# Attention scores without the last key's column, in a key-by-key bank, with a moving operand read by a stride

## The reference

```python
q = split_heads(layernorm(x) @ Wq); k = split_heads(ctx @ Wk); v = split_heads(ctx @ Wv)
attn = softmax(einsum('bhid,bhjd->bhij', q, k) * 64 ** -0.5)          # 77 keys
x = x + tanh(g_xattn[0]) * (merge_heads(attn @ v) @ Wo + bo)
x = x + tanh(g_ffn[0]) * (layernorm(x) @ W[idx] + b[idx])             # one of 8 W, 512 x 512
```

## Time and profile before

| | |
|---|---|
| median of 3 runs | 1053.37 us (1049.84 to 1053.71) |
| profiled execution | 1052.05 us, span 1050.3 us, mean granted TensorE clock 0.998 |
| PE busy | 1035.0 us, 99% of the span, 6065 matmuls |
| DVE busy | 851.7 us, 81% |
| ACT busy | 744.7 us, 71% |
| POOL busy | 438.8 us, 42% |

### The profile page before, as it was taken

The page is one execution under the profiler, slowest core; times in us unless marked ns, Lnnn a source line. Parts: engine busy times, 40 slices in busy tenths (PEclk is TensorE's granted clock), DMA queues, the critical chain, the costliest instruction groups (busy, mean ns, idle before and its releaser), DMA issues.

```text
span 1050.3 us, 21821 instructions
## 1 busy us (share of the span) xinstructions
PE 1035.0 (99%) x6065; PEld 588.1 (56%) x6065; DVE 851.7 (81%) x1800; ACT 744.7 (71%) x2712; POOL 438.8 (42%) x635
## 2 busy tenths in 40 slices
PE   9998899999999999999999999999999999999998
PEld 7634455555555555555555555555555555555555
DVE  4877988888888887888888887888888887888876
ACT  3578887766776677767776677767776676767762
POOL 0575344444433343444433443444433443444322
PEclk9999999999999999999999999999999999999999
DMA  8414466655666656655666656655666656655656
GB/s 312 104 26 107 95 128 133 137 115 117 127 136 135 135 128 134 136 119 110 131 137 135 135 123 139 136 115 110 132 138 137 136 121 135 135 114 113 132 115 141
DMA packets 383639, 135.02 MB, mean 129 GB/s; under 512 B 361728, under 2 KB 363316, under 8 KB 383540
## 3 DMA queue, kind: packets, MB, share of 16 engines
q1 hardware_dynamic: 383476, 134.09, 59.0%
q0 software_dynamic: 64, 0.00, 0.0%
HBM read 27.48 MB, written 16.78 MB: 42 GB/s over the span
## 4 chain that ended last, share of the span: by engine, by line
PE 92%; DVE 4%; ACT 2%; DMA 1%; SPq 1%; issue 1%; POOL 0%; DVEq 0%
PE banks L1356 83%; PE banks L1580 3%; PE banks L1459 1%; PE banks L1386 1%; PE banks L1395 1%; PE banks L1467 1%; ACT work L858 1%; DMA work<-work 1%; DVE vw_area L1062 1%; ACT vw_area L811 1%; PE banks L1448 1%; DVE work L1162 1%; DVE work L425 0%; DMA fold_area<-in_ctx 0%; DVE fold_area L1070 0%
## 5 line engine op out<-in xcount | busy, mean ns | idle before, releaser
L858 ACT ACTIVATE work<-banks,red,cst 128x77 f32<-128x77 f32 x1024 | 410.4, 431 | 89.1 <-DVE red L1153 89.1
L1356 PE MATMUL banks<-fold_area,work 128*128 128x462 f16 (+1 forms) x2304 | 410.6, 336 | 1.4 <-DMA work<-work 0.7
L1356 PE MATMUL banks<-vw_area,work 128*128 128x512 f16 x1674 | 373.1, 380 | 2.6 <-DMA work<-work 2.6
L1356 PEld LDWEIGHTS banks<-fold_area,work 128*128 128x128 f16 x2304 | 223.9, 97 | 176.2 <-DMA work<-work 1.2
L1356 PEld LDWEIGHTS banks<-vw_area,work 128*128 128x128 f16 x1674 | 164.1, 98 | 188.5 <-DMA work<-work 2.9
L425 DVE SCALAR_TENSOR_TENSOR work<-work 128x256 f16<-128x256 f32 (+3 forms) x444 | 240.1, 575 | 3.5 <-ACT work L881 3.0
L858 ACT ACTIVATION_READ_ACCUMULATOR work<-banks,red,cst 128x1 f32 x1024 | 225.7, 220 | 0.0
L1151 DVE TENSOR_REDUCE stats<-banks 128x6 f32<-128x462 f32 (+1 forms) x192 | 112.1, 584 | 109.2 <-PE banks L1356 108.7
L1356 PE MATMUL banks<-work 128*128 128x256 f16 x1302 | 162.4, 272 | 1.6 <-DVE work L1237 1.6
L1356 PEld LDWEIGHTS banks<-work 128*128 128x128 f16 x1302 | 126.7, 98 | 33.4 <-issue 1.3
L703 POOL TENSOR_TENSOR stats<-stats,cst 128x1 f32<-128x1 f32 x64 | 12.5, 196 | 284.7 <-DVE stats L1187 284.7
(11 more groups left out here) (145 smaller groups left out, 814.6 us busy)
## 6 DMA issues: line engine op xcount, KB each, us to landing
work<-in_x SPq DMA_DIRECT2D x64, 256.0 KB, 2.8
out<-work SPq DMA_DIRECT2D x63, 256.0 KB, 2.2
work<-work SPq DMA_TRANSPOSE x254, 3.0
fold_area<-in_L_xattn_Wo SPq DMA_DIRECT2D x4, 512.0 KB, 8.9
work<-in_L_ffn_W SPq DMA_DIRECT2D x2, 1024.0 KB, 6.9
fold_area<-in_L_xattn_Wq SPq DMA_DIRECT2D x2, 1024.0 KB, 12.3
fold_area<-in_L_xattn_Wk SPq DMA_DIRECT2D x2, 768.0 KB, 12.0
fold_area<-in_L_xattn_Wv SPq DMA_DIRECT2D x2, 384.0 KB, 6.2
```

Source lines behind the costliest of these rows:

```text
L858: nc.scalar.activation(probs_of(h, h + 1), s_bank(m, k)[:, (h - h0) * J:(h - h0 + 1) * J], ACT.Exp, bias=nmx[:, h:h + 1], scale=exp_scale, ...
L1356: mm = nc.tensor.matmul(ps, lhs(l), rhs(r), start=first and n == 0, stop=last and n == 2, skip_group_check=onto)
```

## The change

Scores are counted from that of the last key. Before the keys are projected, POOL subtracts the last key's context from that of the 76 others (`ctxT_from_last`), so that `keys_of`, `key_fold` and A carry 76 columns per batch and head in place of 77. The score of the last key is then 0 in every row.

In a score bank the columns now lie key by key: for each key, its 6 (or 4) heads. They end at column 456 in every bank, so that a bank of 4 heads starts at column 152, and columns 456 to 461 of banks 0 to 3 hold zeros, which DVE writes once near the end of the folding. These zeros serve as the last key of all heads. `s_heads` is the view by head of a bank, with its 77 keys. The maxima and the exponentials read through it: successive keys of a head are 6 (or 4) fp32 apart.

A itself stays head by head in SBUF. The score matmul walks it so that its columns come key by key: successive columns are 76 fp16 (152 bytes) apart.

```diff
+    JS = J - 1
+    HS = HEADS * JS
+    BS = B * JS
...
-        a_split = [fold_area[:, k * A_WORDS:(k + 1) * A_WORDS].bitcast(F16)...
+        a_split = [fold_area[:, k * A_WORDS:k * A_WORDS + B * HS].bitcast(F16)...
...
         def s_bank(m, k):
             h0, h1 = BANKS[k]
-            return banks[:, (3 * m + k) % S_BANKS, 0:(h1 - h0) * J]
+            return banks[:, (3 * m + k) % S_BANKS, HB * JS - (h1 - h0) * JS:HB * JS]
+
+        def s_heads(m, k):
+            h0, h1 = BANKS[k]
+            cols = banks[:, (3 * m + k) % S_BANKS, HB * JS - (h1 - h0) * JS:HB * JS + h1 - h0]
+            return cols.rearrange("p (j h) -> p h j", h=h1 - h0)
...
+            for b in range(B):                                     # POOL
+                keys = ctxT[:, :, b * J:(b + 1) * J]
+                pool.wait_ge(ctxT_copied, b + 1)
+                nc.gpsimd.tensor_tensor(ctxT_from_last[:, :, b * JS:(b + 1) * JS], keys[:, :, 0:JS], keys[:, :, JS:J].to_broadcast([P, CT, JS]),
+                                        ALU.subtract).then_inc(ctxT_shifted, 1)
...
-                    nc.scalar.activation(probs_of(h, h + 1), s_bank(m, k)[:, (h - h0) * J:(h - h0 + 1) * J], ACT.Exp,
+                    nc.scalar.activation(probs_of(h, h + 1), s_heads(m, k)[:, h - h0, :], ACT.Exp,
...
+                if (kind, n) == (KEY, UNITS - 3):                  # DVE
+                    assert all(pair_of(KEY, v) >= S_BANKS for v in (UNITS - 2, UNITS - 1))
+                    dve.wait_ge(k_staged, key_staged_before(UNITS))
+                    dve.wait_ge(a_lo, key_highs_after(UNITS - 3))
+                    nc.vector.memset(banks[:, 0:S_BANKS, HB * JS:HB * J], 0.0).then_inc(last_zeroed, 1)
...
-                nc.vector.reduce_max(mx[:, h0:h1], by_head(s_bank(m, k)), AX.X).then_inc(mx_ready, 1)
+                nc.vector.reduce_max(mx[:, h0:h1], s_heads(m, k), AX.X).then_inc(mx_ready, 1)
...
+                if h == 0:                                         # PE, keys_of
+                    pe.wait_ge(ctxT_shifted, B)
-                    mm = nc.tensor.matmul(banks[:, pair_of(PROJECT, h // 2) + h % 2, 0:BJ], wk_raw[:, k, h * P:(h + 1) * P], ctxT[:, k, :],
+                    mm = nc.tensor.matmul(banks[:, pair_of(PROJECT, h // 2) + h % 2, 0:BS], wk_raw[:, k, h * P:(h + 1) * P], ctxT_from_last[:, k, :],
...
-                    nc.tensor.matmul(banks[:, pair_of(KEY, v) + e, 0:BJ], wqT[rows, h, k * P:(k + 1) * P], kT[rows, h, :],
+                    nc.tensor.matmul(banks[:, pair_of(KEY, v) + e, 0:BS], wqT[rows, h, k * P:(k + 1) * P], kT[rows, h, :],
...
+                    if is_tile(o, m, 0) and n == 0:                # PE, scores
+                        pe.wait_ge(last_zeroed, 1)
...
                         mm = split_products(s_bank(m, n), lambda s: turned[:, s, k, :],
-                                            lambda s: a_split[k][:, s, m % B, h0 * J:h1 * J], k == LAST_FOLDED[0], k == LAST_FOLDED[-1])
+                                            lambda s: a_split[k][:, s, m % B, h0 * JS:h1 * JS].rearrange("p (h j) -> p j h", j=JS), k == LAST_FOLDED[0], k == LAST_FOLDED[-1])
```

More of the change, by code:

```diff
@@ L82, in flamingo_layer @@
         fold_area = sb("fold_area", [P, KT * A_WORDS])
-        a_split = [fold_area[:, k * A_WORDS:(k + 1) * A_WORDS].bitcast(F16).rearrange("p (s b n) -> p s b n", s=2, b=B) for k in range(KT)]
+        a_split = [fold_area[:, k * A_WORDS:k * A_WORDS + B * HS].bitcast(F16).rearrange("p (s b n) -> p s b n", s=2, b=B) for k in range(KT)]
         c = Carve(fold_area)
@@ L93, in flamingo_layer @@
         ctxT = c.take(CT * BJ).rearrange("p (k n) -> p k n", k=CT)
+        ctxT_from_last = c.take(CT * BS).rearrange("p (k n) -> p k n", k=CT)
         assert c.at <= 3 * A_WORDS
@@ L153, in flamingo_layer @@
         c.at = folds
-        kT = c.take(HP * BJ).rearrange("p (h n) -> p h n", h=HP)
+        kT = c.take(HP * BS).rearrange("p (h n) -> p h n", h=HP)
         wqT = c.take(HP * D).rearrange("p (h n) -> p h n", h=HP)
-        k_stage = [c.take(2 * BJ).rearrange("p (e n) -> p e n", e=2),
-                   at(D + HP * BJ, 2 * BJ).rearrange("p (e n) -> p e n", e=2)]
-        assert c.at <= x2T_at and D + HP * BJ + 2 * BJ <= RING * D
+        k_stage = [c.take(2 * BS).rearrange("p (e n) -> p e n", e=2),
+                   at(D + HP * BJ, 2 * BS).rearrange("p (e n) -> p e n", e=2)]
+        assert c.at <= x2T_at and D + HP * BJ + 2 * BS <= RING * D
         free = x2T_at + KT * D
@@ L204, in flamingo_layer @@
             sem("ident_zero"), sem("ident_ready"), sem("floor_set"), sem("consts_set"), sem("pads_set"))
-        ctxT_done, ctxT_copied = sem("ctxT_done"), sem("ctxT_copied")
+        ctxT_done, ctxT_copied, ctxT_shifted = sem("ctxT_done"), sem("ctxT_copied"), sem("ctxT_shifted")
         v_done, v_copied, v_scaled, v_scaled_end = sem("v_done"), sem("v_copied"), sem("v_scaled"), sem("v_scaled_end")
@@ L231, in flamingo_layer @@
         s_done, mx_ready, nmx_ready, exp_done = sem("s_done"), sem("mx_ready"), sem("nmx_ready"), sem("exp_done")
+        last_zeroed = sem("last_zeroed")
         rsum_ready, p_ready, p_hi, p_lo, pT_turned, pad_zeroed = (
@@ L393, in pair_banks @@
         def pair_banks(first):
-            return banks[:, first:first + 2, 0:BJ].rearrange("p e (b j) -> p e b j", b=B)
+            return banks[:, first:first + 2, 0:BS].rearrange("p e (b j) -> p e b j", b=B)
         def pair_of_stage(stage):
@@ L402, in pair_of_heads @@
             four, a = h // 2, h % 2
-            cols = a_split[k][:, s, :, 4 * four * J:4 * (four + 1) * J].rearrange("p b (e r j) -> p e b r j", e=2, r=2)
+            cols = a_split[k][:, s, :, 4 * four * JS:4 * (four + 1) * JS].rearrange("p b (e r j) -> p e b r j", e=2, r=2)
             return cols[:, :, :, a, :]
@@ L777, in copy_k @@
                 nc.scalar.copy(kT[:, 2 * n:2 * n + 2, :],
-                               banks[:, pair_of(PROJECT, n):pair_of(PROJECT, n) + 2, 0:BJ]).then_inc(k_copied, 1)
+                               banks[:, pair_of(PROJECT, n):pair_of(PROJECT, n) + 2, 0:BS]).then_inc(k_copied, 1)
             copy_k(0)
@@ L821, in key_high @@
                         act.wait_ge(k_stage_lo, n - 1)
-                    nc.scalar.copy(k_stage[n % 2], banks[:, first:first + 2, 0:BJ]).then_inc(k_staged, 1)
+                    nc.scalar.copy(k_stage[n % 2], banks[:, first:first + 2, 0:BS]).then_inc(k_staged, 1)
                 else:
```

## The result

| | before | after |
|---|---|---|
| median | 1051.95 us (1049.84 to 1053.71, 4 runs) | 2387.68 us (2385.65 to 2389.52, 4 runs) |
| ratio of after to before | | 2.2695, 95% interval 2.2658 to 2.2733 |
| span of the profiled execution | 1050.3 us | 2386.9 us |
| mean granted TensorE clock | 0.998 | 0.657 |

The kernel became 2.27 times as slow. The forecast was 1433 us with a range of 1040 to 1500 us, so the direction was right and the size was not.

What follows compares the result with a forecast made beforehand. PE, busy 99%, was taken as the bound. 1052.05 us + 384 for strided score reads (fewer columns included) - 0.4 key work + 1 PSUM reads + 0.3 memset - 4 covered waits gave 1433 us, range 1040 to 1500 us.

Steps and rivals of the forecast that it cites:

- What bounds the kernel, the columns' gain: PE, busy 99%, sets the loop's time; 192 fewer score columns per tile and smaller key work give -5.5 us.
- The moving operand read with a stride: Score matmuls on PE: neighbouring columns 152 bytes apart share no 4-byte word, adding 384 us over 64 tiles.
- the middle: Strided score read on PE: one word per column, like fp32, 0.833 ns per column, +6.0 us per tile.
- The high end of its own bounds: Strided score read on PE at twice the fp32 rate, 1.67 ns per column, +18.1 us per tile, +1160 us.
- The clock: PE's column price taken at 2.4 GHz; a fall appeared only in a rival, doubling each tile's non-score 8.5 us, +545 us.
- "dearer still" rival: Score read on PE: 1.67 ns or more per column, 2210 us, or the clock falls, 1980 us; chance 0.20.
- Three rivals: Score read on PE: free (1048 us, chance 0.28), partly hidden (1130 to 1360 us, 0.10), or dearer still (0.20).
- The sum's own low bound: Whole kernel at half rate per score column, with nothing of overhead and all covered: 1420 us.
- The reads of PSUM: ACT's exponentials and DVE's maxima read PSUM with a stride; mostly covered, at most 7 us, taken as 1 us.
- The small additions: Before the loop: POOL's four subtractions hidden, up to 6 us without cover; DVE's memset in the folding's chain +0.3 us.
- The covered waits: Near the start PE stands 4.6 us for transpositions; longer scores partly cover this, -4 us.
- the dear case: Sign on PE: a mean distance of 760 ns between score matmuls of 456 columns, against 383 at half rate.

Runs made afterwards that it cites:

- The walk undone: Changed kernel with only the moving operand taking consecutive columns instead of walking by 76 (scores wrong); 1048.19 us, ratio to before 0.996.
- the version with 78 columns: Kernel with 76 columns per head, stored head by head, each head's output run starting every 78 columns, moving operand consecutive; 1046.72 us, ratio to before 0.9955.
- Two, three, four and six places in turn: Kernel before, moving operand taking successive columns from that many separate places in rotation (scores wrong); 0.85, 1.12, 1.69 and 1.79 ns per column.

## Why the prediction was wrong

**What bounds the kernel, the columns' gain.** Right. PE is the limit before and after, and the score column's 0.417 ns stands. The walk undone measured 3.8 us less than before by medians, with the interval 0.27% to 0.52%, 2.8 to 5.5 us, so that the gain of 5.5 us lies at its edge; the version with 78 columns has 5.2 us.

**The moving operand read with a stride.** This step failed, in its choice of the middle: "I take the middle, since its nearest row (the same engine, one word per column) measures just that." It did not. The fp32 rows are consecutive, four words to a line of 16 bytes, and say what a word costs inside a line, not what a new line costs. Nor is that word's price the reading port's: "I read this as a word of 4 bytes delivered per 0.83 ns" is refuted by every 2nd fp16 column, which takes a new word of 4 bytes per 0.44 ns. That fp16 and fp32 had one rate in bytes was no sign of a limit in bytes. The term of 384 us was 1225 us. The high end of its own bounds, 1.67 ns, set as twice the fp32 rate and not from a mechanism, was nearly the measured 1.74. The Trainium skill's figure for VectorE (Vector Engine (DVE) Microarchitecture Reference, Measured stream behaviour on trn2), left out of the sum, was 1.73 ns. PE's 1.74 is near it, which may be chance, since the page speaks of another engine. The Trainium skill's rule of 16-byte lines (Advanced Engine Details and Errata, SBUF Cachelines) agrees with the trace, but its "two hits" per line did not suffice here: two columns per line cost 0.89 ns, four 0.44.

**The clock.** Taken at full in the sum: its fall, 121 us, is the second thing that the sum lacked. It stood only as an alternative inside the "dearer still" rival. Both halves of that rival came, together: 2210 us for the price of the line, and 121 us for the clock. With 1.74 in place of 1.67 ns on 933,888 columns, 65 us more, they give 2396 us against the measured 2387.68. The clock's half was oversized by itself (545 us for all non-score work at half clock), since the clock came back during each attention product (0.62 in its first 3 us, 1.00 after). The rival had the chance 0.20, and the range left it out. Three rivals with no row to part them were a reason for a range that reached it. The sum's own low bound of 1420 us comes to some 1425 by its own terms; nothing hangs on that.

**The reads of PSUM.** Taken at 1 us of a bound of 7: nothing measured, as said.

**The small additions.** POOL's subtraction was hidden: PE's wait for it is not among its waits. PE's wait for DVE's memset is there, 0.9 us once, in place of the 0.67 us of issue that stood at the same place: 0.2 us for the 0.3.

**The covered waits.** The 4.6 us of the earlier trace rows are gone from PE's waits after, as said for 4 of them.

**What would show it.** "760 ns the dear case" was the mark to look for; 25.40 us for 14,592 columns put a matmul of 456 at some 794 ns.

## What to carry to other kernels

The walk of a matmul's fp16 moving operand is priced by the 16-byte lines that it touches in SBUF, at some 1.75 ns each: with fewer than four columns per line the lines set the pace, and at one per line the matmul takes four times as long and the clock falls behind it. Other types were not tried. When a layout has to change between two stages, put neither the hop on PE's input nor single columns on its output: keep runs of four on the input and runs that begin at even words on the output. A row is a price for a new access only if it shares the property that changes; where none does, the range has to hold both ends.

## What the runs showed of the hardware that was not expected

- The price of a line did not depend on the granted clock: four score matmuls in 3.36 us at 1.0 and 3.38 at 0.5.
- Two, three, four and six places in turn cost 0.85, 1.12, 1.69 and 1.79 ns per column (the last with four in every third bank). The rule behind the first two is open.
- An output run that begins at an odd fp32 word costs a little even when it is 76 columns long: 80 ns per 36 matmuls, 0.83 ns for each run with an odd start.
- Strided fp32 reads of PSUM, 16 to 24 bytes apart, are free for ACT and DVE, while fp16 writes to SBUF 32 bytes apart made their instructions 3.6 to 4.3 times as long.
